# Two stages of an eight-part network: expert outputs scattered by token, and the causal mask of a decayed attention moved from TensorE to GpSimd

## The reference, cut to what matters

```
L2_ffn:  pick the 2 best of 8 experts for each token (weights p1, p2), capacity 320 tokens for each expert
         y(token) = p1 * expert1(x) + p2 * expert2(x) + shared(x) + x, then a norm without weights
         expert(x) = (silu(x @ rg) * (x @ ru)) @ rd   with 512 hidden columns; shared: 1024 hidden columns
```

```
L3_attn: s[q, k] = q.k / sqrt(8) (+ decay), -inf for k > q;  softmax over k;  o = s @ v;  x = norm(o @ w_o + x)
L3_ffn:  a ternary weight matrix, a bias and a norm
```

## Time and profile before

| what | value |
|---|---|
| median of 3 runs | 1720.95 us (1720.71 to 1723.78) |
| the profiled execution | 1722.82 us, span 1721.0 us |
| PE busy | 1495.3 us (87%) |
| DVE, ACT, POOL busy | 999.0, 858.4, 643.7 us |
| mean granted clock of TensorE | 0.936 |
| DMA | 64.44 MB, mean 37 GB/s |

### The profile page before, as it was taken

How to read it: one execution, slowest core, us unless ns; L and a number is a source line. 1 busy time by engine, 2 the same in 40 slices (tenths; PEclk the granted TensorE clock), 3 DMA queues, 4 the chain that set the end, 5 groups by cost and what they waited for, 6 DMA issues and landing times. The chain is left out here.

```text
span 1721.0 us, 30934 instructions
## 1 busy us (share of the span) xinstructions
PE 1495.3 (87%) x11187; PEld 1097.3 (64%) x11187; DVE 999.0 (58%) x2358; ACT 858.4 (50%) x1888; POOL 643.7 (37%) x720
## 2 busy tenths in 40 slices
PE   4589999899887999996669999899996899779996
PEld 3256676566764677765647788788784576546664
DVE  6556647665477899983245554466645123445555
ACT  5455555555557877753434444444452132235552
POOL 3387716977133777753110001000013502511113
PEclk8789999999998999997869999999997999879998
DMA  7300000000004866716260000000000201300000
GB/s 217 125 14 13 13 14 1 14 19 13 8 1 77 82 80 79 79 21 163 59 197 6 0 1 1 1 1 0 1 1 10 71 16 34 34 2 2 2 2 25
DMA packets 75919, 64.44 MB, mean 37 GB/s; under 512 B 25627, under 2 KB 63050, under 8 KB 75790
## 3 DMA queue, kind: packets, MB, share of 16 engines
q1 hardware_dynamic: 65790, 54.32, 16.3%
q0 software_dynamic: 3072, 6.30, 1.8%
q10 hardware_dynamic: 6928, 2.12, 0.6%
HBM read 48.88 MB, written 9.58 MB: 34 GB/s over the span
## 5 line engine op out<-in xcount | busy, mean ns | idle before, releaser
L1536 POOL TENSOR_TENSOR inject<-delta_x,b_rows 128x512 f32<-128x512 f32 x128 | 160.1, 1278 | 63.9 <-DVE delta_x L1833 37.5
L1860 DVE TENSOR_TENSOR_SCAN state<-bank,inject 128x512 f32<-128x512 f32 x128 | 150.2, 1210 | 7.5 <-issue 5.2
L2293 POOL TENSOR_TENSOR ve<-mv,eps 128x1 f32<-128x1 f32 x32 | 6.1, 190 | 335.6 <-DVE mv L2441 335.6
L1765 ACT ACTIVATE bank<-delta,a_neg 128x255 f32<-128x255 f32 x256 | 109.2, 473 | 7.4 <-DVE state L1860 6.7
L3556 DVE TENSOR_REDUCE top<-bank 128x2 f32<-128x512 f32 (+1 forms) x96 | 61.8, 685 | 71.5 <-PE bank L3258 50.9
L2402 ACT ACTIVATE Z<-bank 128x512 f32<-128x512 f32 x64 | 34.7, 595 | 128.9 <-PE bank L2355 128.9
L2379 ACT ACTIVATE U<-bank 128x512 f32<-128x512 f32 x128 | 74.6, 593 | 40.7 <-PE bank L2316 39.6
L1640 PEld LDWEIGHTS bank<-tabs,by_token 128*128 128x128 f32 x512 | 68.3, 197 | 24.9 <-issue 15.1
L628 POOL TENSOR_TENSOR rotated<-rot_cos,rot_sin 128x512 f32<-128x512 f32 x52 | 65.8, 1268 | 46.0 <-DVE rot_sin L997 46.0
L634 POOL TENSOR_TENSOR inv_norm<-sum_sq,neghalf 128x16 f32<-128x16 f32 x26 | 76.2, 2929 | 3.9 <-POOL sum_sq L632 0.8
L1776 ACT ACTIVATE by_token<-bank,c_cols 128x256 f32<-128x256 f32 x128 | 53.6, 470 | 46.4 <-PE bank L1614 46.1
(11 more groups left out here) (572 smaller groups left out, 4152.8 us busy)
## 6 DMA issues: line engine op xcount, KB each, us to landing
b_rows<-rows_dram SPq DMA_DIRECT2D x32, 512.0 KB, 9.1
v<-v SPq DMA_DIRECT2D x32, 130.0 KB, 2.3
slots<-zero SPq DMA_DIRECT2D x10, 256.0 KB, 4.3
rows<-slots SPq DMA_DIRECT2D x10, 256.0 KB, 4.2
moe_w<-in_L_ffn_rg_dram SPq DMA_DIRECT2D x1, 2048.0 KB, 8.7
moe_w<-in_L_ffn_ru_dram SPq DMA_DIRECT2D x1, 2048.0 KB, 14.0
wqkv<-in_L_ffn_wqkv_dram SPq DMA_DIRECT2D x2, 768.0 KB
slots_out<-y SPq DMA_DIRECT2D x8, 160.0 KB, 2.1
```

The costliest lines, as they stand in the source:

```text
L1536: pool.tensor_tensor(dB[:, n % R, :, :], dx[:, :, seq(n)], both(b_all[:, q % 4, n % CH, :]), ALU.mult).then_inc(s.inject.sem, 1)
L1765: last = act.activation(dA[n % RD][:, c, 1:L], delta[:, c, i * L + 1:(i + 1) * L], ACT.Exp, scale=a_neg[:, c, k:k + 1])
L1860: dve.tensor_tensor_scan(flat(h[:, n % R, :, :]), flat(dA[n % RD]), flat(dB[:, n % R, :, :]), 0.0, ALU.mult, ALU.add).then_inc(s.state.sem, 1)
```

## The change

It has three parts.

**Memory.** The first block writes zeros over `slots0` only. The first layer's SP list gains, behind its last small move, six DMAs of zeros for `padded` (a slot array whose rows have 129 numbers), eight for `by_token`, and one DMA that writes a number into the last column of each of the 2560 slots; it waits for them before `ready_next`.

**Experts.** Each scattered row carries its token number in column 129. ACT first makes two such copies of x (four instructions of 128 x 1024). The 32 scatters now go to `padded`. POOL reads the numbers back as `ids`. Three shared pairs stand ahead of the experts and one behind. After each expert POOL scatters its rows straight to their tokens in `by_token`, 20 indirect DMAs in all (five tiles for each two experts), and SP then loads `by_token` in token order with 16 plain DMAs. `combine(0)` stands between chunks of the last pair, the others behind it. `gather` and the 32 indirect gathers are gone.

**Attention.** `mask` is gone. POOL sets the probabilities above the diagonal to zero after the exponential (`causal(i, c)`, two AFFINE_SELECT instructions of 128 x 4 x 128), and `mix` waits for that. DVE copies the first two quarters of k and q out of PSUM (`copy_first`), and ACT the last two.

```diff
@@ stage_recurrence
-                for buf in net.slots:
+                for buf in net.slots[0:1]:
@@ first_layer, sync
                 att1.on_sync(sp)
+                for at in range(0, KT * ROW, width):
+                    end = min(at + width, KT * ROW)
+                    sp.dma_start(rows[:, at:end], net.zero[:, 0:end - at]).then_inc(net.fetched, 16)
+                for at in range(0, 2 * NT * D, width):
+                    sp.dma_start(tokens[:, at:at + width], net.zero[:, :]).then_inc(net.rows_in, 16)
+                    sp.dma_start(net.padded[0:SLOTS, D:ROW].rearrange("(k p) o -> p (k o)", p=P), spare[:, :]).then_inc(net.fetched2, 16)
@@ stage_top2_experts
-                shared_expert(0, PAIRS // 2)
+                shared_expert(0, FIRST)
...
-                shared_expert(PAIRS // 2, PAIRS)
+                shared_expert(FIRST, PAIRS)
@@ vector
-                shared_pair(PAIRS // 2)
-                for i in range(3):
-                    combine(i)
-                shared_pair(PAIRS // 2 + 1)
-                for i in range(3, EARLY):
+                shared_pair(FIRST, 0, SC - 2)
+                combine(0)
+                shared_pair(FIRST, SC - 2, SC)
+                for i in range(1, EARLY):
                     combine(i)
@@ gpsimd
+                for e in range(E2):
+                    q = e // 2
+                    pool.wait_ge(s.y_sb.sem, s.y_sb.at(0, e + 1))
+                    for tile in ((0, 1), (2, 3, 4))[e % 2]:
+                        pool.indirect_dma_start(net.by_token, bass.IndirectOffsetOnAxis(ap=ids[:, at:at + 1], axis=0),
+                                                y[:, q % 2, tile, :], None).then_inc(stored[q % 2], 16)
@@ sync
+                for half in stored:
+                    sp.wait_ge(half, 16 * PER * E2 // 4)
+                for i, done in enumerate(arrived):
+                    of = slice(TPB * i, TPB * (i + 1))
+                    for c in range(2):
+                        sp.dma_start(both[:, c, of, :], by_tile[:, c, of, :]).then_inc(done.sem, 16)
@@ decayed_attention_and_ternary, gpsimd
+                def causal(i, c):
+                    pool.wait_ge(s.exped.sem, s.exped.at(i, HPG * (c + 1)))
+                    for at in (0, L):
+                        of = prob[:, c, :, at:at + P]
+                        last = pool.affine_select(of, of, [[0, HPG], [1, P]], ALU.is_ge, pool.to_reg(0.0), base=0, channel_multiplier=-1)
+                    last.then_inc(s.causal.sem, 1)
@@ tensor
                 def mix(i, p, half):
-                    pe.wait_ge(s.exped.sem, s.exped.at(i, 2 * HPG * (half + 1)))
+                    pe.wait_ge(s.causal.sem, s.causal.at(i, 2 * (half + 1)))
@@ scalar
-                        for m in range(4):
+                        for m in (2, 3):
                             copy_qk(i + 1, 1 - p, m)
@@ vector
                     if ahead:
+                        copy_first(i + 1, 1 - p)
```

More of the change, by code:

```diff
@@ L2997, in _, with shared_pair @@
                 weights()
-                def shared_pair(i):
-                    for c in range(SC):
+                def shared_pair(i, first=0, end=SC):
+                    for c in range(first, end):
                         dve.wait_ge(s.s_silu.sem, s.s_silu.at(i, c + 1))
@@ L3147, in decayed_attention_and_ternary @@
         turn_bank = lambda m: X[1 - m % 2]
+        copied = lambda i, m: (s.qk_first if m < 2 else s.qk_second).at(i, m % 2 + 1)
+        copies = lambda m: (s.qk_first if m < 2 else s.qk_second).sem
         def runs(run):
@@ L3170, in _, with cast @@
             def _(pool):
-                def cast(i, p):
+                def causal(i, c):
[4 more added lines that the diff above has]
+                    last.then_inc(s.causal.sem, 1)
+                def cast(i, p, first=0):
                     pool.wait_ge(s.scored.sem, s.scored.at(i, 0))
-                    for m, (which, t) in enumerate(TURN):
+                    for m, (which, t) in enumerate(TURN[first:first + 2], first):
                         to, of = (k16, kT[p]) if which == "k" else (q16, qT[p])
-                        pool.wait_ge(s.qkT.sem, s.qkT.at(i, m + 1))
+                        pool.wait_ge(copies(m), copied(i, m))
                         settle(pool, s)
@@ L3179, in run @@
                 def run(i, p, ahead, behind):
-                    if ahead:
-                        cast(i + 1, 1 - p)
+                    causal(i, 0)
+                    cast(i + 1, 1 - p)
+                    causal(i, 1)
+                    cast(i + 1, 1 - p, 2)
+                    causal(i, 2)
+                    causal(i, 3)
                     if behind:
@@ L3204, in _ @@
                 cast(0, 0)
+                cast(0, 0, 2)
                 for i in range(B - 1):
                     run(i, i % 2, min(2, B - 1 - i), i > 0)
-                for k in range(B - 2):
-                    tern_rstd(k)
+                causal(B - 1, 0)
+                causal(B - 1, 1)
+                tern_rstd(0)
+                tern_rstd(1)
+                causal(B - 1, 2)
+                tern_rstd(2)
+                tern_rstd(3)
+                causal(B - 1, 3)
+                tern_rstd(4)
+                tern_rstd(5)
                 norm_rstd(pool, s, n, B - 2)
@@ L3357, in run @@
                     shifted(i, p, 1)
-                    mask(i, 1)
                     if behind:
@@ L3547, in rotate, with copy_first @@
                         dve.tensor_tensor(dst[:, :, 2:4, :, 1], prod[:, 2, :, :, :], prod[:, 3, :, :, :], ALU.add).then_inc(s.wide.sem, 1)
+                def copy_first(i, p):
+                    for m in range(2):
+                        which, t = TURN[m]
+                        dve.wait_ge(s.turned.sem, s.turned.at(i, m + 1))
+                        to = kT[p] if which == "k" else qT[p]
+                        dve.tensor_copy(to[:, :, tok(t)], turn_bank(m).rearrange("p (c t) -> p c t", t=P)).then_inc(s.qk_first.sem, 1)
                 def highest(i, u):
```

142 lines of the change are left out of this document (78 added, 64 removed).

## The result

| | before | after |
|---|---|---|
| median, same chip | 1722.37 us (1720.71 to 1724.35, 4 runs) | 1698.67 us (1696.52 to 1700.92, 4 runs) |
| ratio | | 0.9861, 95% interval 0.9845 to 0.9877 |
| profiled execution, span | 1722.82, 1721.0 us | 1698.1, 1696.3 us |
| mean granted clock of TensorE | 0.936 | 0.939 |

The median of the changed kernel is 23.7 us lower: 1698.67 us, where 1701.8 was forecast. The span of the trace is 24.7 us shorter. Where they lie is read from the starts of the stages: the first instruction of each, in both traces.

What follows compares the result with a forecast made beforehand. No single engine bounds it all: SP's list ends the first block, gathers the experts tail, PE is busy 143.2 of 158.8 us in attention. 1721.0 - 3.4 - 5.5 - 10.3 = 1701.8 us, range 1690 to 1716.

Steps and rivals of the forecast that it cites:

- Memory, -3.4: First block: SP's list ends it, so dropping five of ten zero DMAs saves their whole 3.43 us.
- The cover in the first layer: First layer: new zeros and 2560 small writes have 61 us of cover less 4.3, so cost nothing unless writes exceed 45.
- Experts, -5.5: Experts stage: Silu -0.5, pairs -2.7 and tail -2.3 us; bounds -14 and +3 by an unexplained stall.
- The Silu's -0.5: Experts stage: DVE loses two small links ahead of the routing weights ACT's first Silu waits for, saving 0.5 us.
- 2.3 forecast: Experts tail: combines end with PE, combine 6 ends 0.7 earlier and combine 7 follows without its 1.64 us wait: -2.3 us.
- pairs, -2.7: Shared pairs after the change: one ahead (21.8) and one behind (23.1), 44.9 us against 47.5 for two behind today.
- so even half as long again: Experts stage: PE asks for scattered rows a pair later, so scatters of 68 us for 45 would cost a microsecond or so.
- The stall at 1350 goes: Rival, experts stage: ACT's 9.63 us wait before 1359.83 vanishes since instruction lists shift: 1693.2 us, chance 0.09.
- Attention, -10.3: Decayed attention: 1.6 us saved a batch over seven batches, -11.2, less 0.9 lost in the last batch.
- a of 0.85: Attention: assumed time of one POOL select in us, between the one-input rows and the two-input row (1.27).
- PE's own 2.0: Attention: without mask and q wait, PE reaches the second mix 2.0 us earlier per batch if nothing else is late.
- 3.3 - 2a: Attention: saving of a batch in us when two POOL selects of length a precede the second mix; at most 2.0.

Runs made afterwards that it cites:

- rest_only: Kernel before with only the memory and experts parts of the change, attention as it was: 1711.39 us against 1725.07, ratio 0.9926.
- two_ahead: Changed kernel with two shared pairs ahead of the experts and two behind, as before the change: 1709.74 us, ratio 0.9888 to the kernel before.
- pair_moved: Kernel before with only the third shared pair moved ahead of the experts, gathers kept: 1756.01 us against 1729.78, ratio 1.0154.
- att_only: Kernel before with only the attention part (selects on POOL, DVE's first two copies): 1715.04 us against 1725.07, ratio 0.9944.
- before_again: Kernel before, unchanged, run again for a second trace: 1733.97 us, one run.
- sel_only: Changed kernel with the selects, but all four q and k copies on ACT as before: 1711.76 us, ratio 0.9896 to the kernel before.
- scatter_late: Changed kernel with POOL's scatters of token rows held back until ACT has copied the first shared pair: 1708.64 us, one run.
- act_shift: Changed kernel with 20 tiny copies more on ACT at the start of the experts stage: 1704.52 us, one run.
- sel_spare: Changed kernel with a second, unread select ahead of each select: 1718.43 us against 1729.75 for the kernel before, ratio 0.9943.
- after_again: Changed kernel, unchanged, run again beside the kernel before on the same chip: 1702.52 us against 1725.77, ratio 0.9852.

## Why the prediction was right, and where it was not

**Memory, -3.4.** The mechanism was right: SP's list ended the block and still does. In this pair of traces 2.5 came, since the five zero DMAs took 10.07 us here and not 8.95. That is chance: the first five take 9.0 to 11.2 us over all traces, but the five behind them 3.2 to 3.4, and the mean start of the next block moves by 3.4, as forecast. In the profiled execution after, the slow spell at 584 took the gain back; rest_only kept it. The cover in the first layer held.

**Experts, -5.5.** The Silu's -0.5 came as 0.6 (PE's first wait is 1.33 for 1.95). The last combine waits for no DMA, and the end behind PE is 2.5 shorter for 2.3 forecast. The first combine comes 11.3 us after the last y, 11.4 forecast. The term "pairs, -2.7" was wrong in its reason. A pair with another behind it costs 22.9, not 21.8, so a moved pair is worth nothing by itself (two_ahead, with the stall in both traces). The pairs' part came out at 1.5, from gaps that went with the gathers. All of the tail's 4.0 us, 60.6 to 56.6 in two_ahead, belongs to the outputs written by token; pair_moved shows that without that the moved pair is lost time.

The step that failed is the one on the scatters: PE asks for the rows a pair later, "so even half as long again" would cost little. I looked only for a cost there. In the kernel before PE would have waited 5.5 us for the rows, and 2.8 more went with the clock behind the wait (att_only); the stall hid both in the one trace that I had. The third pair ahead covers this wait. In traces of like condition the stage is therefore shorter by 13.0 us (no stall in either, att_only and rest_only on one chip) or by 9.5 (the stall in both, before_again and sel_only on two chips), not by the 5.5 forecast or the 4.6 that pairs, tail and Silu gave. The "microsecond or so" was too low as well: the rows landed 8.3 us behind the end of the last scatter (scatter_late, 88.9 and 80.6 us into the stage), so scatters of 68 us would have had them there at some 85.6, where PE asked at 77.3, an estimated 8 us of waiting. They took 44 us, so nothing came of it.

**The stall.** "The stall at 1350 goes" was a rival, with 0.09. It did go in this trace, but not because instruction lists shift (act_shift). And its 8.6 us were not to be had: without the stall the kernel before waits for its rows and takes as long, 187.2 us (att_only) for 187.3.

**Attention, -10.3.** It gave 12.3. My a of 0.85 was too high, since the select takes only 0.02 more than the cast's 0.61. At 0.634 the selects just fit (POOL ends 0.18 us before PE asks), so what bounds the saving is its upper limit, PE's own 2.0, and not 3.3 - 2a. Measured is 1.88: 1.8 and 0.74 won, 0.66 lost. Where POOL does bound the batch the formula held, 0.76 for 0.73 in sel_spare. The Trainium skill (GPSIMD Engine Reference, 4.1 Engine selection) was the better guide: by its one-input rule I had 13.6, nearer to the 12.3 than my 10.3 (the time by it is 1698.5 us, not 1698.4). The page compares GpSimd with VectorE; here that is 1.27 us on POOL for 0.69 on DVE with two inputs (L628, L994 in the kernel before), and 0.61 for 0.69 with one (POOL's cast, DVE's copy). The batches save 12.6 in seven, the last one costs 0.2 where 0.9 was forecast, and the first `turn_top` comes 0.1 later.

**The sum.** Between the two traces lie -2.5 (memory), -13.1 (experts), -12.3 (attention) and +3.2 (the slower clock in the scan stage), together -24.7. The forecast had -3.4, -5.5 and -10.3, together -19.2. So the experts' part was forecast at under half its size and the attention's 2.0 too small. That the total came so near, 1698.67 for 1701.8 us in the medians, is in part luck: the slow spell of 3.2 us, the 0.9 of memory and a median before that had itself moved from 1720.95 to 1722.37 us stood against them. The ratio repeats: 0.9861, 0.9863 (with ten zeros, on the chip where no trace has the stall) and 0.9852 (on the chip of after_again, where all three traces, of the changed kernel and its variants, have it).

## What to carry to other kernels

Before costing an order of work, ask what a stall in the only trace may be hiding: take it out of the sum and see which wait comes next, and whether the clock falls behind that wait. Moving independent work to the front pays only where something else waits there, and only if what stands behind does not wait for a fixed chain such as gathers. A causal mask on probabilities can go to an idle POOL as long as two selects fit between the last exponential and the product that reads it.

## What the runs showed of the hardware

- An affine select on POOL takes 0.634 us for 128x512 numbers, a cast of the same shape 0.61; doubled back to back, 0.638 each.
- While POOL's indirect scatters run, ACT takes two results of PE late (waits of 6.1 to 7.9 and 8.3 to 12.5 us for the usual 4.3 and 3.6; with the scatters 27 us later it was the second pair, 6.7 and 6.9, and once the third, 7.5 for 5.4). It was in all nine traces of three chips, in none of the three of a fourth, and in one of the first two; PE loses 8.6 to 14.8 us. Moved scatters move it; a longer ACT list does not. The first copy beside the gathers of the kernel before was late too (8.0 and 8.2 us for 4.3, before and before_again), where the stage was no longer for it. The 20 scatters of the changed kernel's expert loop did nothing of the kind: the loop takes 60.0 us in all ten traces.
- Behind 2.4 and 1.2 us of idle PE at the rows the granted clock was 0.50 for some 4 us, and the expert loop took 2.8 us longer (att_only, one trace).
- TensorE's half-clock spells differ between executions of identical instructions: up to 4 us in the scan stage (273.0 to 277.1 over the traces), up to 7 from the third layer to the experts (537.0 to 544.1).
- Five DMAs of 256 KB of zeros, queued behind 6 MB of weights, took 9.0 to 11.2 us over the traces; the next five, where there were ten, 3.2 to 3.4.
